# One program for four stages of a two-layer graph attention kernel, weights and rows of the second layer read ahead, and row tiles split ahead of keys and query sums

## What is computed

```python
def _gat_layer(x, W, adj):
    proj = x @ W
    Wh, Ws = jnp.split(proj, 2, axis=-1)
    scores = Wh @ Ws.T
    a = jax.nn.softmax(scores, axis=-1) * adj
    out = a @ Wh
    out = out + x
    return jax.nn.leaky_relu(out, NEG_SLOPE)
# x = _layernorm(x + the layer above, twice over, of x)
# out = adj @ (max(sign(x), 0) @ sign(weight).T)
# x = _layernorm(x + relu(out))
```

## Time and profile before

| | us |
|---|---|
| median of 3 runs (2334.63 to 2335.42) | 2334.77 |
| the profiled execution | 2334.61 |
| its span, first to last instruction | 2332.8 |
| PE busy with products | 2132.3 (91%) |
| DVE busy | 1539.2 (66%) |
| ACT busy | 920.3 (39%) |
| POOL busy | 725.0 (31%) |
| mean granted clock of PE | 0.97 |

### The profile page before, as it was taken

One profiled execution on the slowest core, in us unless ns is written; L12 is line 12 of the kernel. 1 busy time (PEld: TensorE's weight loads), 2 busy tenths in 40 slices (PEclk: granted clock), 3 DMA queues, 4 the chain that ended last, 5 costly groups with the idle time before them and its releaser, 6 DMA issues. The chain is left out here.

```text
span 2332.8 us, 38788 instructions
## 1 busy us (share of the span) xinstructions
PE 2132.3 (91%) x13260; PEld 1297.2 (56%) x13260; DVE 1539.2 (66%) x3933; ACT 920.3 (39%) x2071; POOL 725.0 (31%) x677
## 2 busy tenths in 40 slices
PE   3996999999999999994985999999999999997699
PEld 1443666666666666661333666666666666664244
DVE  3664677777777777774564577666666776676254
ACT  5663433444444343333564334443333444332000
POOL 1783222232222232221673333332222333231000
PEclk9998999999999999997997999999999999998799
DMA  5887667777877766764887778778677877865775
GB/s 176 170 172 165 138 149 153 152 153 155 156 158 149 150 148 146 154 129 127 199 185 170 156 163 162 160 164 174 139 159 163 162 160 164 174 137 132 247 249 180
DMA packets 735312, 378.99 MB, mean 162 GB/s; under 512 B 642064, under 2 KB 655376, under 8 KB 733456
## 3 DMA queue, kind: packets, MB, share of 16 engines
q1 hardware_dynamic: 724304, 340.77, 64.6%
q0 software_dynamic: 3328, 22.16, 6.5%
q10 hardware_dynamic: 7488, 13.63, 1.8%
HBM read 204.60 MB, written 59.64 MB: 113 GB/s over the span
## 5 line engine op out<-in xcount | busy, mean ns | idle before, releaser
L791 PE MATMUL p_out_a<-values,probs_t_a 128*128 128x512 f16 x4056 | 957.9, 379 | 0.4 <-DVE acc_a L998 0.4
L767 PE MATMUL p_scores_a<-keys_t,q_t_a 128*128 128x256 f16 x6552 | 812.9, 275 | 54.6 <-DMA q_t_a<-values 33.8
L921 POOL TENSOR_TENSOR row_a<-row_a,adj_rows_a 128x512 f32<-128x512 f32 (+1 forms) x364 | 456.3, 1268 | 1229.1 <-ACT row_a L877 1211.9
L767 PEld LDWEIGHTS p_scores_a<-keys_t,q_t_a 128*128 128x128 f16 x6552 | 642.2, 99 | 250.5 <-DMA q_t_a<-values 34.8
L791 PEld LDWEIGHTS p_out_a<-values,probs_t_a 128*128 128x128 f16 x4056 | 396.9, 98 | 372.3 <-DVE acc_a L998 0.9
L869 ACT ACTIVATE row_a<-p_scores_a 128x256 f32<-128x256 f32 x468 | 177.8, 380 | 727.1 <-PE p_scores_a L767 725.5
L979 DVE SCALAR_TENSOR_TENSOR halves_a<-row_a,halves_a 128x512 f16<-128x512 f32 (+1 forms) x364 | 278.3, 765 | 200.2 <-ACT halves_a L890 197.7
L500 PE MATMUL p_rows_p<-w_p,x_t_p 128*128 128x512 f16 x1248 | 279.4, 384 | 88.7 <-DMA x_t_p<-x_p 88.5
L877 ACT ACTIVATE row_a<-row_a,shift_a,scales 128x512 f32<-128x512 f32 (+1 forms) x364 | 281.1, 774 | 148.7 <-DVE shift_a L969 148.3
L998 DVE SCALAR_TENSOR_TENSOR acc_a<-acc_a,factor_a,p_out_a 128x512 f32<-128x512 f32 x312 | 232.8, 746 | 128.9 <-PE p_out_a L791 123.9
L934 DVE CUSTOM_DVE_ANT_0 row_a<-row_a,p_scores_a 128x256 f32<-128x256 f32 x468 | 196.1, 419 | 129.8 <-PE p_scores_a L767 106.0
(11 more groups left out here) (101 smaller groups left out, 1377.9 us busy)
## 6 DMA issues: line engine op xcount, KB each, us to landing
adj_rows_a<-adj_rows SPq DMA_DIRECT2D x312, 256.0 KB, 3.2
adj_t<-adj_blocks POOLq DMA_DIRECT2D x104, 208.0 KB, 3.8
adj_b<-adj_t SPq DMA_DIRECT2D x26, 832.0 KB, 4.4
s_rows<-sum_rows_p SPq DMA_DIRECT2D x26, 512.0 KB, 2.9
x_rows_a<-x_rows SPq DMA_DIRECT2D x52, 256.0 KB, 3.4
values<-x_rows SPq DMA_DIRECT2D x13, 512.0 KB, 5.4
adj_rows_a<-adj_rows SPq DMA_DIRECT2D x52, 128.0 KB, 2.6
x_mid<-work_a SPq DMA_DIRECT2D x26, 256.0 KB, 3.4
```

The source lines that it names most:

```text
L767: last = pe.matmul(bank(w, name), queries(pair_of(w), q_block, qh, c), keys_t[:, kh, k_block, c, cols], start=(first and c == 0 and n == 0 ...
L791: last = pe.matmul(p_out[:, u], probs_t[:, turned_slot(w), u, ph * tiles + j, :], values[:, 4 * step_of(w) + j, vh, :], start=(j == 0 and ...
L921: pool.tensor_tensor(piece, piece, adj_rows[:, n % ADJ_RING, 0:width(w)], ALU.mult).then_inc(masked, 1)
```

## The change

The first four stages become one block. `project` and `attend` now return functions, one for each engine, and every engine runs `project`, `attend`, `project`, `attend` in a row with no barrier. PSUM is one tensor of eight banks for all four stages, and SBUF tensors are laid by hand into one area, where tensors of neighbouring stages share bytes; waits on the last user stand where a barrier did. Further:

- The start of `attend` no longer waits for all of `project`: the first queries are turned by SP between the last row tiles, and the work on the last pair (values, keys and sums: `act_tail`, `dve_tail`, `sp_tail`) is placed inside windows 0 and 1.
- The weights of layer 1 are loaded during attention 0 in 8 pieces, twice: once for the maximum (`see_piece`) and once to be split (`piece_hi`, `piece_lo`), at steps 1 and 4 of pairs 1 to 4 and 6 to 9. The maximum is spread by POOL after the masks of window 34 (`spread_w_peak`), and DVE makes the scale in window 35 (`scale_w`).
- The rows of layer 1 are loaded in the last windows of attention 0, and the first three tiles are split and turned there.
- Row scales come from the exponent bits by four DVE operations (`top_over_root`) with no square root and no maximum; that maximum (`scale_layer`) is needed only before the first `copy_rows`.
- In the projections ACT and DVE split a row tile ahead of the keys or sums of the pair behind.
- `sign_product` comes after the first two products of its window. The signs of `weight` are made in window 3.
- POOL's wait for the casting transfers is at the end of layer 1 alone. `dynamic_dma_scratch_size=4096` is given where nothing was.

The diff, cut to its core:

```diff
-            for layer in range(LAYERS):
-                project(nc, sems, layer, layer_in, w_stack, kept, values, keys_t, keys_last, s_rows, T, DC, D)
-                attend(nc, sems, layer, layer_in, x, adj, layer_out, kept, values, keys_t, keys_last, s_rows,
-                       weight, products_kept, adj_t, adj_t16, N, NP, T, DC, D, last)
+            with nc.Block() as block:
+                @block.sync
+                def _(sp):
+                    for layer in range(LAYERS):
+                        projects[layer]["sp"](sp, attends[layer]["turn_first_queries"])
+                        attends[layer]["sp"](sp)
...
+    def see_piece(dve, k):
+        dve.wait_ge(w_loaded, 16 * (k + 2))
+        dve.reduce_max(facts[:, 12 + k:13 + k], w_piece[:], AX_X, apply_absolute_value=True).then_inc(w_seen, 1)
+    def spread_w_peak(pool):
+        pool.wait_ge(w_peak, layer + 1)
+        pool.partition_all_reduce(facts[:, 1:2], facts[:, 0:1], P, REDUCE_MAX).then_inc(w_peak_all, 1)
+    def scale_w(dve):
+        chain.link(dve.memset(exponent[:], EXPONENT_BITS))
+        dve.wait_ge(w_peak_all, layer + 1)
+        chain.link(dve.tensor_scalar(facts[:, 2:3], facts[:, 1:2], LEAST_BOUND, None, ALU.max))
...
+    def top_over_root(dve, out, squared_norms, spare):
+        bits = spare.bitcast(U32)
+        chain.link(dve.tensor_scalar(spare, squared_norms, LEAST_BOUND * LEAST_BOUND, None, ALU.max))
+        chain.link(dve.tensor_scalar(bits, bits, 24, None, ALU.logical_shift_right))
+        chain.link(dve.tensor_scalar(bits, bits, -1.0, TOP_OVER_ROOT, ALU.mult, ALU.add))
+        return dve.tensor_scalar(out.bitcast(U32), bits, 23, None, ALU.logical_shift_left)
...
+    def sp_program(sp, turn_first_queries):
...
+        else:
+            load_x(sp, J - 1)
+        for i in range(J):
+            if i >= 3:
+                turn_keys(sp, i - 3)
+            if layer == 0 or 2 * i >= X_RING:
+                turn_x(sp, 2 * i)
+            if i >= 3:
+                store_sums(sp, i - 3)
+            if layer == 0 or 2 * i + 1 >= X_RING:
+                turn_x(sp, 2 * i + 1)
+            if i >= J - 3:
+                turn_first_queries(sp, i - J + 3)
+        turn_keys(sp, J - 3)
+        store_sums(sp, J - 3)
...
+        act.wait_ge(evict_ready, layer + 1)
+        for i in range(J):
+            for two in (0, 1):
+                copy_rows(2 * i + two, 0)
+                if 2 * i + X_RING + two < T:
+                    x_hi_half(act, 2 * i + X_RING + two)
+                if i >= 1:
+                    (keys_hi_half, sums_hi_half)[two](act, i - 1)
+                copy_rows(2 * i + two, 1)
...
+            for two in (0, 1):
+                if 2 * i + X_RING + two < T:
+                    x_lo_half(dve, 2 * i + X_RING + two)
+                if i >= 1:
+                    (keys_lo_half, sums_lo_half)[two](dve, i - 1)
...
+    for n in range(2 * pieces):
+        piece_windows[STEPS * (1 + n // 2 + n // pieces) + (1, 4)[n % 2]] = n
...
+            elif u == 0:
+                sp.wait_ge(values_lo, first_pair + J)
+                sp.wait_ge(sums_stored, 16 * (first_pair + J))
...
+                behind = w - (windows - STEPS) - LAG - 1
+                if w >= windows and w - windows < X_RING:
+                    ahead["turn_x"](sp, w - windows)
+                if 0 <= behind < WIDE:
+                    ahead["load_x"](sp, 2 * behind)
+                    ahead["load_x"](sp, 2 * behind + 1)
...
-                    for t, at in made_now:
-                        sign_product(t, w)
                     if w >= windows:
                         pass
                     elif wide(w):
...
                         strassen(w, SET_A, A11, B11 - 1, True)
                         free(w, 1)
                         strassen(w, SET_B, A12, B21 - 1, True)
                     else:
                         free(w, 3)
                         plain(w, SET_A, 0)
+            for t, u in made_now:
+                sign_product(t, w)
                     mix(w - LAG, 0, 0)
...
+            if w == 0:
+                now["act_tail"][1](act, J - 1)
...
+            if ahead and piece_windows.get(w - 2, -1) == pieces - 1:
+                ahead["spread_w_peak"](pool)
...
+            if w == 1:
+                now["dve_tail"][2](dve, J - 1)
...
-                    if last_layer and w == 1:
+            if last_layer and w == 3:
                 make_signs()
...
-    nc = bacc.Bacc("TRN2", target_bir_lowering=False, num_devices=1)
+    nc = bacc.Bacc("TRN2", target_bir_lowering=False, num_devices=1, dynamic_dma_scratch_size=4096)
```

More of the change, by code:

```diff
@@ L36 @@
 EXPONENT_BITS = 0x7F800000
+TOP_OVER_ROOT = 203.0
 def ceil_div(a, b):
@@ new lines, with attend @@
+SET_A, SET_B, SET_E = 0, 1, 2
+def attend(nc, sems, layer, layers, dram, kept, held, small, at, now, ahead, N, T, DC, D):
+    norms2, var_eps, adj_low = (kept[n] for n in ("norms2", "var_eps", "adj_low"))
+    scales = kept["scales"][:, layer]
+    values, keys_t, keys_last, banks = (held[n] for n in ("values", "keys_t", "keys_last", "banks"))
+    adj, adj_t, adj_t16, s_rows, x_first = (dram[n] for n in ("adj", "adj_t", "adj_t16", "s_rows", "x_first"))
+    last_layer = ahead is None
+    x_in = x_first if layer == 0 else dram["x_mid"]
+    rows_out = dram["centred"] if last_layer else dram["x_mid"]
+    weight, products_out = dram["weight"], dram["products"]
@@ new lines, in bank, with out_bank, quarter, as_quarter @@
+    def bank(w, name):
+        return banks[:, (4, 0)[w % 2] + name, 0:2 * P]
+    def out_bank(u):
+        return banks[:, 3 + 4 * u]
+    def quarter(w, u, odd):
+        return row[:, slot(w), u].rearrange("p (j e q) -> p e j q", e=2, q=P)[:, odd]
+    def as_quarter(ap):
+        return ap.rearrange("p (j q) -> p j q", q=P)
+    def queries(i, block, half, c):
+        places = {A11: 4 * half, A12: 4 * half + 2, A21: 8 + 4 * half, A22: 8 + 4 * half + 2}
+        at_chunk = places[block] if block in places else 16 + 8 * half + 2 * (block - S1)
+        return q_t[i % 2][:, at_chunk + c, :]
```

1590 lines of the change are left out of this document (841 added, 749 removed).

## The result

The changed kernel takes 2267.4 us (median of 4 runs, 2265.4 to 2270.6), the kernel before, on the same chip, 2335.1 (4 runs, 2334.6 to 2337.5). The ratio is 0.971, with a 95% interval of 0.969 to 0.973: 68 us less, where 91 were forecast. The time lies 1.4 us above the range.

The account below looks back on a forecast made before the run. PE's order and waits were taken to bound the attention bodies, with mostly empty seams between stages. Nine stage terms summed to 2241.9 us; with 1.8 around the span and 0.2 for the median, 2244 us, range 2224 to 2266.

Parts of the forecast that it names:

- Projections: Both projections: splitting the row tile first removes PE's waits for it; 143.5 to 139.8 and 152.4 to 138.4 us.
- The seams: Last row product to first mix, both layers: 26.0 of windows plus 2.5 of last-pair work; 28.5 and 28.2 us.
- the seams are refilled: Rival, both attention seams: last-pair work holds up windows 0 and 1 by its full 9.0 us; 2257 us, chance 0.1.
- Seam into projection 1: Attention 0 to projection 1: 34.1 us falls to 0.5, at worst 5, with the fourth tile just in time.
- Attention 0: Its body: weight pieces cost nothing, POOL's code change near window 35 costs 10 us (bounds 0 and 20); 826.0 to 836.0.
- several holes at the pieces: Sign of being wrong: several PE holes in attention 0 where the pieces of the weights are handled.
- the code change is cheap: Rival, attention 0: code changes of 6 us or less cost 0 to 4 more, not 10; 2236 us, chance 0.15.
- the row tiles stay late: Rival, projections: SP's transposes set the pace, so waits of 4.2 and 12.0 us stay; 2259 us, chance 0.1.
- Sign products: Body of attention 1: issued behind two score products, they leave 2 of 16.5 us waiting; 860.6 to 843.5 us.
- The rival that the wait is for the turned bits: Attention 1: the sign products' wait is not for the accumulation and moves along; 2261 us, chance 0.06.
- The slow rival: Casting transfers get less descriptor space and POOL stands until they land; at 11 us each about 2390 us, chance 0.02.
- A seam that stays: Rival: a wait on a last user replaces the barrier, so one seam of 17 us stays; 2261 us, chance 0.05.

Follow-up runs that it names:

- the last version: Changed kernel with key rows copied before value rows, weight pieces moved, maxima spread through DRAM in later windows, SP load moved, fourth tile split earlier: 2224.3 us.
- keys first: Changed kernel, but ACT copies the key rows of both tiles of a pair before the value rows of either: 2239.0 us, ratio 0.958.
- queries turned last: Changed kernel, but SP turns the first three query blocks behind the last row tile, not behind the last three pairs: 2266.0 us, ratio 0.970.

## Why the prediction was wrong, step by step

- **Projections, the step that failed.** "Both engines now split the tile first, so that wait no longer lies on it." That is so, and yet 3.3 and 6.7 us came of it, and then with a bill in the seams. What was not walked is what stands behind the wait. ACT's order has another wait in each pair, for POOL's sums in front of the single buffer `vb`. In the kernel before it was hidden under the wait for keys (4.2 us over both projections). With the key wait gone, and DVE's key operation pushed to where it meets POOL's query sums, it is up to 4.4 us in nearly every pair, 86.2 in all with the seams. "139.8" and "138.4" took PE as the only bound left. With the ring broken, the kernel gives 137.8 and 139.3: the forecast was about right for a kernel in which POOL is not in the way. Its floors were not PE's own, though. Taking only the waits off 143.5 left 139.3 (and 137.4 in projection 1), and the last version needs 134.8 for the same 624 products.
- **The seams, 1.7 and 6.4 us.** I split them into 26.0 of windows and 2.5 of last pair. The 26.0 was no floor: without the ring they take 23.2 and 26.6 in all. 2.2 us of it was the lower clock: PE's first 30 score products took 5.71 us behind 17 us of standing still, at a granted clock of 0.59, and 3.51 at 1.00 in "keys first". The overrun was the projections' ring again, not the last pair's six halves. The rival "the seams are refilled" named the right place with the wrong filling.
- **Seam into projection 1.** Right: no wait at the first product, and the tile that was late is the fourth, by 2.8 us and not 0.5. The copy ahead of it was not the only reason: the wait stayed when the tile was split first, and went when SP's load ahead of the transposes was moved as well.
- **Attention 0.** Forecast 10.0 over 826.0, measured 10.7, but made up of two parts, which cost 6.6 (the change of code) and 4.8 (the pieces) when each is taken away. The pieces I had cost at nothing, and the code at 10, since I put the masks 11.7 us late where they were 7.3. That the total fits is luck: the single hole of about 10 us did not come, and the sign of being wrong that I gave, several holes at the pieces, did. The cover that I named, DVE's idle time of 204 us over the body, was a mean over windows; the pieces stood in front of the one window that has none.
- **The price of the change of code.** I took the one loaded case, 9.49, against about 6 of the Trainium skill ("GPSIMD Engine Reference", section 2.1). The trace has 7.10 and 6.92, so for one change the page was nearer. For PE's loss neither was: my 10 is 3.4 over the measured 6.6, and the 3 to 4 that the page's figure gives is about as far under it. The rival "the code change is cheap", with 0 to 4, falls with it. The code changes once more ahead of the first key sums of projection 1 (6.99 us); no wait of PE goes back to it.
- **The rival "the row tiles stay late"** had the right rows and the wrong engine. SP's queue is 1.2 us of one wait and up to 2.7 us of projection 0 with the clock ("queries turned last"), and the fourth tile of projection 1; POOL and ACT are the rest.
- **Sign products.** Right: 17.1 forecast, 16.5 in the stage, 14 to 16 as a part alone. The rival that the wait is for the turned bits falls. 4.7 us of it is left and 0.5 of a wait for DVE, not 2.
- **Casting transfers.** The slow rival had no part: POOL's 104 issues took 59.0 us before and 59.2 after.
- **A seam that stays.** None did: no seam shows the 17 us of that rival.
- **The range** reached to one rival and a bit. Two stages of one kind shared one wrong step, so the misses came together: 5.6, 8.0, 1.7 and 6.4. The bounds for the projections (139.3 to 143.5, 137.4 to 152.4) did not even hold projection 0, since I had let the order of before be its upper end: a change of order can add a wait too.

## What to carry to other kernels

When a wait goes, walk the whole loop of the engine that had it, and ask of each other wait in it how long it would be if the first were not there; an engine that is idle 40% of a stage can still be in a ring through a single buffer. To break a ring, look first for two steps in it that need not be in that order: two copies exchanged gave 28 us here, more than what the reordering in the change had given (5.7 between the medians, with intervals that overlap). Work put "in idle time" has to be placed by window, not by the mean, and that goes for small transfers too.

## What the runs showed of the hardware that was not expected

- **DVE lengthens POOL's operations.** A POOL sum of 128x256 takes 0.71 to 0.74 us by itself, and 2.38 to 2.50 beside DVE's 128x1792 subtraction; which sum is hit depends only on the place. The rows give a rule. In projection 1 of the changed kernel, from 1062 us on, 54 sums start while a DVE operation with two inputs from SBUF runs, more than 0.08 us after its start, and every one of them ends 0.57 to 0.60 us after that operation ends. So a sum costs what is left of the DVE operation, and not a share of it. It holds the other way too: DVE's low half of a row tile takes 0.75 us while POOL has nothing to do (1060.09) and 1.21 to 1.33 beside its sums (1149.09, 1144.51). The eight sums of all pairs took 218.0 us before and 249.3 after (the totals of their lines), and 210.9 with that DVE operation cut. The Trainium skill has the rule ("GPSIMD Engine Reference", section 8, Key points): POOL shares its SBUF interfaces with VectorE, and DVE instructions with two SBUF inputs contend. The trace agrees; I had not used it.
- **A small transfer can be slow and hold up others.** 0.5 KB from 128 partitions took 9.4 us to land (8.7 to 9.4 in four kernels), where a load of 256 KB takes 3.2 in the median, and such a load issued behind it landed about 2.5 us late. Moved by three windows it made no hole of PE.
- **A change of POOL's code** took 7.1 and 6.9 us beside the attention's transfers, and 9.49, the maximum included, in the case seen before. A third stands between the norms' maximum (1055.89) and the first key sum of projection 1 (1063.26): POOL stands 6.99 us, though the last copy that this sum needs had ended at 1061.1.
